# Staging the layer norm over four tiles, storing a tile with one DMA, and adding scan outputs in pairs

## The reference, cut to what matters

```python
xn = layernorm(x)                                 # over 1024 channels
x = x + mamba(xn) + bitlinear_ffn(xn)

# mamba: 2048 inner channels, 16 states, chunks of 256 tokens
xc, res = split(xn @ W_in.T + b_in)
u = silu(causal_conv3(xc))
dlt, Bm, Cm = split(u @ W_x.T)                    # 64, 16, 16
delta = softplus(dlt @ W_dt.T + b_dt)
dA = exp(delta * -exp(A_log)); dBu = delta * Bm * u
h[t] = dA[t] * h[t-1] + dBu[t]                    # starts at 0 in each chunk
y[t] = sum over 16 states of h[t] * Cm[t]
out = (y * silu(res)) @ W_out.T + b_out

# ffn: activations rounded to 8 bits by row, weights to -1, 0, 1 by tensor
gate = silu(q8(xn) @ tern(w_gate).T); up = q8(xn) @ tern(w_up).T
out = q8(gate * up) @ tern(w_down).T
```

## Time and profile before

| | us |
|---|---|
| median of 3 runs | 5382.02 |
| lowest, highest | 5379.02, 5385.85 |
| the profiled execution | 5377.95 |
| its span (slowest core) | 5376.0 |
| DVE busy | 3918.5 (73%) |
| ACT busy | 1865.0 (35%) |
| PE busy | 1641.5 (31%) |

### The profile page before, as it was taken

The page is one execution under the profiler, slowest core; times in us unless marked ns, Lnnn a source line. Parts: engine busy times, 40 slices in busy tenths (PEclk is TensorE's granted clock), DMA queues, the critical chain, the costliest instruction groups (busy, mean ns, idle before and its releaser), DMA issues.

```text
span 5376.0 us, 45957 instructions; the slowest of 8 cores (5339.2 to 5376.0 us)
## 1 busy us (share of the span) xinstructions
PE 1641.5 (31%) x7308; PEld 829.0 (15%) x7308; DVE 3918.5 (73%) x10735; ACT 1865.0 (35%) x4106; POOL 211.3 (4%) x380
## 2 busy tenths in 40 slices
PE   0013410321050032105003310500200167786776
PEld 0002200110030011003001100300000023333332
DVE  2332888888888888888888888888888666664232
ACT  1234434343433444343332432333222122224332
POOL 1450000000000000000000000000000000000000
PEclk9997655655575565557556555755555588998998
DMA  5512202310330141033002100300100133330666
GB/s 181 184 52 81 63 0 80 94 34 0 102 106 0 43 129 36 0 102 114 0 0 67 47 0 0 114 0 0 47 0 0 71 119 99 121 93 20 208 207 195
DMA packets 316918, 378.34 MB, mean 70 GB/s; under 512 B 19346, under 2 KB 257042, under 8 KB 314516
## 3 DMA queue, kind: packets, MB, share of 16 engines
q1 hardware_dynamic: 296596, 316.68, 19.6%
q0 software_dynamic: 18304, 46.16, 2.3%
q10 hardware_dynamic: 1728, 12.58, 0.7%
HBM read 329.22 MB, written 46.14 MB: 70 GB/s over the span
## 4 chain that ended last, share of the span: by engine, by line
DVE 43%; issue 16%; PE 15%; DMA 14%; ACT 9%; DVEq 1%; POOL 1%; SPq 0%; ACTq 0%; POOLq 0%
DVE hbuf L658 18%; DVE dbub L651 8%; DVE ypb L672 6%; ACT dAb L642 4%; DMA wdqt<-s_wdq 3%; DVE yA L675 3%; PE psBC L621 3%; PE psBC L628 2%; DMA wo_buf<-s_woutT 2%; DMA s_wdq<-wdstg 2%; PE psB L1089 1%; DMA wqf<-wuT 1%; PE psC L1089 1%; DMA wch<-s_winT 1%; PE psG L911 1%
## 5 line engine op out<-in xcount | busy, mean ns | idle before, releaser
L658 DVE TENSOR_TENSOR_SCAN hbuf<-dAb,dbub 128x256 bf16<-128x256 bf16 x2048 | 1399.8, 683 | 164.8 <-ACT dAb L642 164.8
L675 DVE TENSOR_TENSOR yA<-yA,ypb 128x256 f32<-128x256 f32 x1920 | 816.2, 425 | 203.9 <-DVE ypb L672 6.0
L642 ACT ACTIVATE dAb<-delta_t,alneg 128x256 bf16<-128x256 bf16 x2048 | 905.4, 500 | 48.1 <-DVE hbuf L658 46.5
L621 PE MATMUL psBC<-shstB,ones 1*128 1x256 f32 x256 | 148.9, 682 | 2063.1 <-DVE shstB L618 2063.1
L632 ACT ACTIVATE Bsb<-psBC 128x256 bf16<-128x256 f32 x128 | 49.0, 383 | 1924.0 <-PE psBC L628 1869.5
L651 DVE TENSOR_TENSOR dbub<-du_t,Bsb 128x256 bf16<-128x256 bf16 x2048 | 581.2, 284 | 5.9 <-ACT Bsb L632 2.4
L672 DVE TENSOR_TENSOR ypb<-hbuf,Csb 128x256 bf16<-128x256 bf16 x1920 | 511.5, 266 | 0.0
L621 PEld LDWEIGHTS psBC<-shstB,ones 1*128 1x128 f32 x256 | 62.1, 299 | 2117.3 <-issue 2117.3
L491 PE MATMUL psI<-xnsc,wch 128*128 128x256 bf16 x2048 | 326.9, 328 | 152.9 <-DMA wch<-s_winT 141.0
L491 PEld LDWEIGHTS psI<-xnsc,wch 128*128 128x128 bf16 x2048 | 229.3, 117 | 255.3 <-issue 196.2
L725 PE MATMUL psOut<-wo_buf,gated 128*128 128x512 bf16 x256 | 114.0, 445 | 446.6 <-DVE gated L697 384.4
(11 more groups left out here) (148 smaller groups left out, 3239.0 us busy)
## 6 DMA issues: line engine op xcount, KB each, us to landing
wch<-s_winT SPq DMA_DIRECT2D x128, 512.0 KB, 4.5
wdqt<-s_wdq SPq DMA_DIRECT2D x64, 1024.0 KB, 6.7
wo_buf<-s_woutT SPq DMA_DIRECT2D x64, 512.0 KB, 4.3
wab<-wgT SPq DMA_DIRECT2D x32, 512.0 KB, 4.4
wab<-wuT SPq DMA_DIRECT2D x32, 512.0 KB, 4.4
wab<-wdT SPq DMA_DIRECT2D x32, 512.0 KB, 4.2
wqf<-wgT SPq DMA_DIRECT2D x64, 256.0 KB, 3.4
wqf<-wuT SPq DMA_DIRECT2D x64, 256.0 KB, 3.4
```

The costliest lines, as they stand in the source:

```text
L621: P.op("tensor", lambda t, bk=bk: t.matmul(psBC[bk][:, 0:CH], ones2[64:65, 0:128], shstB[64:65, :], start=True, stop=True), reads=["shB", ...
L642: P.op("scalar", lambda s, q=q, n=n, b=b: s.activation(dAb[b][:], delta_t[p][:, q * CH:(q + 1) * CH], AF.Exp, bias=0.0, scale=alneg[:, q * ...
L658: P.op("vector", lambda v, b=b, b3=b3: v.tensor_tensor_scan(hbuf[b3][:], dAb[b][:], dbub[b3][:], 0.0, ALU.mult, ALU.add), reads=["dA:%d" % ...
L675: P.op("vector", lambda v, q=q, b=b: v.tensor_add(yA[:, q * CH:(q + 1) * CH], yA[:, q * CH:(q + 1) * CH], ypb[b][:]), reads=["yA:%d" % q, ...
```

## The change

Three things change. The layer norm's operations of one tile, now 40, are cut at positions 3, 10 and 20 into four pieces, and round j emits piece 0 of tile j, piece 1 of tile j-1, piece 2 of tile j-2 and piece 3 of tile j-3. The eight stores of a copy become one DMA of 256 KB with the same 256-byte runs in DRAM. In the scan, rows 1, 3, ..., 13 put their product into one of 16 new buffers `pa`; rows 2, 4, ..., 14 add `pa` to their product in bfloat16 and add the sum to `yA`. Rows 0 and 15 stay as they are.

```diff
-    def ln_gen():
-        for i in range(NT + 1):
+    def _tile_ops(i):
+        if True:
...
-                    for kb in range(8):
-                        yield lambda b=b, kb=kb, dstd=dstd, i=i, tg=tg: P.op(
-                            "gpsimd", lambda e: e.dma_start(
-                                dstd.ap()[kb * 128:(kb + 1) * 128, i * 128:(i + 1) * 128],
-                                trev[b][:, kb * 128:(kb + 1) * 128]),
...
+                    yield lambda b=b, dstd=dstd, i=i, tg=tg: P.op(
+                        "gpsimd", lambda e: e.dma_start(
+                            dstd.ap()[:, i * 128:(i + 1) * 128].rearrange(
+                                "(k part) c -> part k c", k=8),
+                            trev[b][:].rearrange("part (k c) -> part k c", k=8)),
...
+    def ln_skewed():
+        tiles = []
+        for i in range(NT):
+            it = _tile_ops(i)
+            tiles.append([fn for fn in it])
+        cuts = (0, 3, 10, 20, None)
+        for j in range(NT + 3):
+            for st in range(4):
+                i = j - st
+                if 0 <= i < NT:
+                    a, b = cuts[st], cuts[st + 1]
+                    for fn in tiles[i][a:b]:
+                        yield fn
+        for fn in _tile_ops(NT):
+            yield fn
...
+    pa = [salloc(mstk, "pa%d" % i, [128, CH], BF16) for i in range(16)]
...
+            elif n % 2 == 1 and n != 15:
+                P.op("vector", lambda v, q=q, b3=b3, e2=e2: v.tensor_mul(
+                    pa[q][:], hbuf[b3][:], Csb[e2][:]),
+                    reads=["h:%d" % b3, "Csb:%d" % e2], writes=["pa:%d" % q])
             else:
                 P.op("vector", lambda v, q=q, b=b, b3=b3, e2=e2: v.tensor_mul(
                     ypb[b][:], hbuf[b3][:], Csb[e2][:]),
                     reads=["h:%d" % b3, "Csb:%d" % e2], writes=["yp:%d" % b])
+                if n % 2 == 0:
+                    P.op("vector", lambda v, q=q, b=b: v.tensor_add(
+                        ypb[b][:], ypb[b][:], pa[q][:]),
+                        reads=["yp:%d" % b, "pa:%d" % q], writes=["yp:%d" % b])
```

More of the change, by code:

```diff
@@ L390, in ln_gen @@
                         reads=["psT:%d" % tp], writes=["trev:%d" % b])
-                    for kb in range(8):
-                        yield lambda b=b, kb=kb, dstd=dstd, i=i, tg=tg: P.op(
-                            "gpsimd", lambda e: e.dma_start(
-                                dstd.ap()[kb * 128:(kb + 1) * 128, i * 128:(i + 1) * 128],
-                                trev[b][:, kb * 128:(kb + 1) * 128]),
-                            reads=["trev:%d" % b],
-                            writes=["%s:%d:%d" % (tg, kb, i)], dma=True)
+                    yield lambda b=b, dstd=dstd, i=i, tg=tg: P.op(
[3 more added lines that the diff above has]
+                            trev[b][:].rearrange("part (k c) -> part k c", k=8)),
+                        reads=["trev:%d" % b],
+                        writes=["%s:%d:%d" % (tg, kb, i) for kb in range(8)], dma=True)
             else:
@@ L408, in ln_gen @@
                     reads=["psT:0"], writes=["xnh_fm"])
+    def ln_skewed():
[13 more added lines that the diff above has]
+            yield fn
     _wc = iter(wcast_gen())
-    _ln = iter(ln_gen())
+    _ln = iter(ln_skewed())
     while True:
```

## The result

| | before | changed |
|---|---|---|
| median of 8 runs, us | 5381.49 | 5211.52 |
| lowest, highest | 5372.98, 5385.85 | 5205.06, 5217.17 |
| ratio, 95% interval | | 0.9685 (0.9674 to 0.9695) |
| profiled execution | 5377.95 | 5210.04 |

The kernel is 170 us faster. I had forecast 90 us, 5292, with a range of 5218 to 5345. Both parts gave about twice what I had worked out, and rival A is not the reason, as the experiments show.

The account below looks back on a forecast made before the run. DVE was taken to pace the scan and a chain of waits the layer norm, with the `w_inT` piece bound by loads. -50 and -40 us from 5377.95 gave 5288, plus 4 for the median: 5292, range 5218 to 5345.

Parts of the forecast that it names:

- rival A: In the scan, the loads keep up when ACT asks sooner: gain 50 + 117 = 167, time 5215, chance 0.12.
- A round of the layer norm: ACT's chain per round in the layer norm: 13.7 us against 16.23, and 17.5 beside the weight tiles.
- the term L: ACT's pause in the layer norm until the first copy's stores land: 5.0 us, bounds 2.8 and 7.1.
- a price per weight tile: In the layer norm's `w_outT` part, each weight tile adds 1.4 us, 3.8 us a round.
- The `w_inT` part: Layer-norm piece while the eight `w_inT` tiles pass: taken as bound by its loads, end left at 151 us.
- The pairs' own gain: In the scan, a pair of bodies falls from 3.02 to 2.88 us, 0.14 each: -117 us before charges.
- rival C: In the scan, the bfloat16 addition in place runs at the float32 rate, 0.42: time 5435, chance 0.05.
- What is taken back: Charges on the scan's gain where ACT or loads hold odd rows: 28 + 36 + 14 us, leaving -39.
- f0_abs: Scan charge: its loads at 1.55 us a body hold the odd rows in chunks 0 to 3, +28 us.
- pre_a_mm: Scan charge: matmuls waiting for `wch` hold ACT in rows 3 and 1, +36 us.
- the even row gives nothing back: In the scan, where ACT or a load sets the pace, the odd row's loss is not recovered in the even row.
- post_out: Scan charge: row 1's first four odd bodies lie beside DVE's wait for output matmuls, 2 us in seven chunks, +14.

Follow-up runs that it names:

- e5_loads_sp: The kernel before with the odd weight tiles' loads issued by SP instead of ACT: 5353.8 us, 0.9964 of the kernel before.
- e12_no_wo: The changed kernel with wo_buf loads only for chunk 0's output; its rival was that wch holds row 1: 5177.8 us, 0.9643 of the kernel before.
- e1_ln_only: The changed kernel without the pairs in the scan, so only the new layer norm: 5279.6 us, 0.9823 of the kernel before.
- e2_pairs_only: The changed kernel with the layer norm as before, so only the pairs in the scan: 5290.6 us, 0.9851 of the kernel before.
- e3_stage_only: The kernel before with only the layer norm's staging over four tiles, eight stores a copy kept: 5346.2 us, 0.9947 of the kernel before.
- the shifted pairs: The changed kernel with the pairs of odd q shifted by one state, state 1 alone: 5179.9 us, 0.9646 of the kernel before.

## Why the prediction was wrong, point by point

**A round of the layer norm.** The links were right and the term L was mis-sized: 3.92 us for 5.0 in the last rounds. I took the median landing of the `s_woutT` stores, 4.5, which come from the busy part; the single stores landed in 3.7 and 3.3 at the median, and in 3.2 at the least. Over the 7.8 rounds behind the weights that is 8 us. By the Trainium skill ("DMA: Bandwidth & Descriptors", anatomy of one DMA) L would have been 3.1, an estimate, too low by 0.8 us where I was too high by 1.1. Beside the `w_outT` tiles a round took (223.11 - 131.94) / 6 = 15.2 us and not 17.5, 14 us in six rounds. There I had added a price per weight tile taken from the kernel before; in the trace after, the pauses of these rounds are 4.4 to 7.6 us, 2.5 above the last rounds' on the mean, so most of the price is a longer wait for the store, once a round.

**The `w_inT` part.** The failed step is "I take that piece as bound by its loads", with its end left at 151 us. It ended at 132.5. The 70% and 244 GB/s of the earlier trace rows were a mean over loads that came late: ACT's issues stood behind second copies that waited up to 32 us for eight stores, and those stores behind a weight tile's. `e5_loads_sp` shows it alone: 85% and 23 us. In the changed kernel the longest such wait up to the last `w_inT` load is 16.4 us. This term is 18 us. With the 8 and 14 above it makes the 40 us missing in the layer norm.

**The pairs' own gain.** 0.14 us a pair and 2.1 a pair of rows were measured as -1.9 to -2.0 where nothing holds the rows. Over 56 pairs of rows that is 108 to 112 us, so -117 nearly stands as the sum without charges, and rival C is out: the addition takes 0.29. The Trainium skill ("VectorE: DVE Perf Modes", section on mode 2x_1P) had that right. C's own sum was a little off: with 0.42 for the addition an even body comes to 2.03, not 2.04, and the pairs cost 134 us more, not 143.

**What is taken back.** I charged 78 us; 117 - 90 = 27 were taken, or about 20 against the measured gain of a pair. For `f0_abs` I charged 28, and leaving its loads out gives 18 back. The mechanism is there: the odd row wants to run at 1.0 us a body and with the loads it takes 1.5 (row 13 of chunks 1 to 3: 23.6 us for 16 bodies; without the loads 20.2). For `pre_a_mm` I charged 36, and the test gives 8. One failed step is the reading of the earlier trace rows as a pace of 18.8 us for "14 bodies". The stretch holds 16 `dAb`: the next copies of B and C stand before q = 2 of row 4, so its last two are row 4's. To the last `dAb` of row 3 it is 17.1 us, and a charge of 3.1. It was also one row of one core, core 0 in chunk 1, and it counted the two copies of B and C at its start. Core 4 of the same execution, same row, has

```profile
1079.47 0.38 ACT L632 ACTIVATE Bsb<-psBC 128x256 bf16<-128x256 f32 x1 [10.46 <-DVE dbub L651]
...
1095.04 0.50 ACT L642 ACTIVATE dAb<-delta_t,alneg 128x256 bf16<-128x256 bf16 x1
```

16.1 us from end to end for the same 16, and 14.9 for row 3's own 14. From the end of the first of these 14 to the end of the last, core 4 needs 13.9 to 16.3 us over chunks 1 to 6 in the kernel before, and DVE's 13 odd bodies 12.8. The other number in my own text, 1.07 a body at best from the drained loads, would have given 1 us a row; row 3 lost 1.7, for it fell by 5.3 us where row 5 fell by 7.0.

The second failed step in this term is "the even row gives nothing back". Row 4 grew by 3.5 us where row 6 grew by 5.2, so it gave the 1.7 back, and rows 3 and 4 together cost the change next to nothing: -1.8 against -1.9 to -2.0. Beside the `wab` loads the sentence held: row 14 grew by 5.0 in chunks 1 to 3 and in chunks 4 to 6. Why the two places differ was not tried.

For `post_out` I charged 14 us on the ground that DVE's wait for the matmuls is fixed in time and swallows what row 1 gains. Row 1 fell from 28.4 to 20.6 us, more than the 7.0 of row 5, and the wait for `mmo` went from 33.7 to 38.1 only; its part in row 1 went from 2.0 to 2.2 us a chunk on the mean of the cores. The wait in row 1 was not fixed by the `wo_buf` loads: with them left out row 1 is the same. Without the `wch` loads it falls from 2.3 (the changed kernel again) to 1.7 us, and row 1 by 0.9, so the rival named before `e12_no_wo` ran has a part in it. What the rest hangs on was not tried further.

**Rival A** would have needed `wab` and `wch` to keep up; `wab` did not. The measured 5211 comes from -90 in each part and +10 behind the scan, not from -50 and -117. The lower end of my range rested on no sum: the 5242 before it takes 60 us for the scan, where my own bounds for that part were 15 and 117, and 5218 was set so as to leave A out.

**Open.** The stages behind the scan take 10 us longer on the mean of the cores (1114 to 1124), 8 of it by the end of the gate and up projections. `e1_ln_only` shows 2 us of it, `e2_pairs_only` 3, and the changed kernel run again 7. By the end of those projections alone the two with the pairs stand 7 us above the kernel before and `e1_ln_only` stands level with it; but `e3_stage_only`, without the pairs, stands 4 us above it, so that the pairs delay these stages is not shown. No experiment was aimed at it, and I have no cause.

## What to carry to other kernels

In this kernel a DMA share of 70% in a stage with several issuing queues was no sign of a limit: look at which instruction of the issuing engine stands ahead of each load, and how long it waits. When work is made uneven on the bounding engine, ask which other engine or load has a pace between the fast and the slow piece, and price it from several cores and chunks, not from one row, with the pieces in the stretch counted; spreading the fast and slow pieces evenly, as the shifted pairs do, gave 21 us at no operation more. A staged pipeline is only as good as its last shared buffer: here one `trev` for two copies cost 3.9 us a round, and a second one gave 45 us.

## What was not expected of the hardware

A GpSimd DMA of 1024 runs of 256 bytes kept POOL for 0.89 us and landed in 3.3 to 3.7, against 0.54 and 1.8 for 128 runs; eight times the runs, and the bytes, cost 0.35 us of issue and 1.5 to 1.9 of landing. A bfloat16 addition in place whose one operand was just written took 0.29 us where the products took 0.27.
